# First recurrent stage of a four-layer network: one multiply moves to GpSimd, one gate moves into PSUM, and the second layer runs two chunks behind

## The chip, the cores and the metric

The kernel runs on one core of a Trainium2 chip. A core has a matrix engine (TensorE, PE in the rows), VectorE (DVE), ScalarE (ACT), GpSimd (POOL), a queue that starts transfers (SP), an on-chip memory SBUF that all of them reach, and PSUM, eight banks of 512 fp32 columns by 128 partitions into which TensorE writes. The metric is the device time of one execution in microseconds (us); lower is better. The time before is the median of three runs.

## The reference, cut to what matters

The program computes eight sublayers, each followed by a residual add and a layer norm. Only the first is touched: two minGRU layers, one after the other, over 4 sequences of 1024 tokens with 128 features.

```python
def _mingru_train(x, Wz, bz, Wh, bh):
    k = jnp.einsum('bsi,hi->bsh', x, Wz) + bz
    log_z = -jax.nn.softplus(-k)
    log_coeffs = -jax.nn.softplus(k)
    log_tilde_h = _log_g(jnp.einsum('bsi,hi->bsh', x, Wh) + bh)
    ...
    log_h = a_star + jax.lax.cumlogsumexp(log_values - a_star, axis=1)
    return jnp.exp(log_h)[:, 1:]
...
h1 = _mingru_train(x, Wz0, bz0, Wh0, bh0)
h2 = _mingru_train(h1, Wz1, bz1, Wh1, bh1)
...
x = _layernorm(x + h2, axis=-1)
```

Out of the logarithm this is h[t] = a[t] h[t-1] + z[t] g[t] with z = sigmoid(k), the update gate; a = sigmoid(-k) = 1 - z, the decay; and g, the candidate, which is max(u + 0.5, sigmoid(u)) for u = Wh x + bh. The state starts at 0.5 in each sequence.

## The kernel before, in words

The program is a list of parts (`stage1`, a fence, the first layer norm, a fence, `stage2`, ...). Each part gives each engine its own instruction stream; semaphores (`Sig` objects) order work between engines, and a fence lets no engine into the next part until four engines have drained. Within an engine instructions run in the order in which they are written.

`stage1` cuts the 4096 tokens into 8 chunks of 512 (two to a sequence) and does each chunk in each of the two layers l: 16 items (l, i), in the order of the list `seq`; p is an item's place in it. For each item

- TensorE projects the chunk with Wz and Wh into two PSUM banks, `PS[2 * (p % 4)]` and the one behind it. An fp32 product of 512 columns is two MATMUL rows in the trace, so one item is four MATMUL rows. Items of layer 1 read the states of layer 0 in `H1`.
- ScalarE (`scalar`) evaluates three sigmoids: a into `Ba`, z into `Bz`, sigmoid(u) into `Bs`. In the rows they are L203 with ps,SM (a) and ps,W (z and sigmoid(u)).
- VectorE (`dve`) forms the candidate g (L211), multiplies it by z (L208), and runs the recurrence as one scan instruction (L432), into `H1` or `Bh`.
- GpSimd (`pool`) adds the states of layer 1 to the residual stream `XT` (L212), 8 adds in all.

`Ba` to `Bh` have three buffers each, and PSUM holds the projections of four items. `seq` puts layer 1 of chunk i behind layer 0 of chunk i + 1. The first layer norm begins behind the fence, so behind the last of the eight adds.

Of the kernel before, what the change touches and what calls it, by code (L numbers as in the profile page):

```python
# [8 lines left out]
ALU = mybir.AluOpType  # L9
ACT = mybir.ActivationFunctionType  # L10
# [7 lines left out]
NCH = T // CH  # L18
# [114 lines left out]
def ch(ap, i, k=CH):  # L133
    return ap[:, i * k:(i + 1) * k]
# [16 lines left out]
def of(plan, step):  # L151
    return [a for s, a in plan if s == step]


def build(nc, wp, xT_d, sidx_d, cs_d, vecs_d, out_d):
# [3 lines left out]
    sem = Semaphores(lone)  # L159
# [21 lines left out]
    PS = [PSALL[:, i * 512:(i + 1) * 512] for i in range(8)]  # L181

    def w(name):
        r, o, c = at[name]
        return W[0:r, o:o + c]
# [5 lines left out]
    def mm(out, lhsT, rhs, start=True, stop=True, **k):  # L191
        return nc.tensor.matmul(out, lhsT, rhs, start=start, stop=stop, **k)  # L192
# [8 lines left out]
    def act(out, x, f, bias=0.0, scale=1.0, acc=None):  # L201
        if acc is None:
            return nc.scalar.activation(out, x, f, bias=bias, scale=scale)  # L203
        return nc.scalar.activation(out, x, f, bias=bias, scale=scale, accum_out=acc)  # L204
# [3 lines left out]
    tt = lambda o, a, b, op: nc.vector.tensor_tensor(o, a, b, op)  # L208
    ts = lambda o, a, s1, s2, op0, op1=None: (nc.vector.tensor_scalar(o, a, s1, s2, op0, op1) if op1 is not None  # L209
                                             else nc.vector.tensor_scalar(o, a, s1, None, op0))  # L210
    stt = lambda o, a, s, b, op0, op1: nc.vector.scalar_tensor_tensor(out=o, in0=a, scalar=s, in1=b, op0=op0, op1=op1)  # L211
    gtt = lambda o, a, b, op: nc.gpsimd.tensor_tensor(o, a, b, op)  # L212
# [37 lines left out]
    for k in LN_ALONE:  # L250
        p = ln_plans[k] = [("centre", (k, 0)), ("centre", (k, 1))]
# [108 lines left out]
    def stage1():  # L360
        ar = arena()
        H1 = ar(T)
        Ba, Bz, Bs, Bg, Bh = ([ar(512) for _ in range(3)] for _ in range(5))
        nb, bh5 = SM[:, 64:66], SM[:, 66:68]
        b = w("b_l0a")
        b2 = b.rearrange("p (l k) -> p k l", k=2)
        seq = []
        for i in range(NCH + 1):
            seq += [(0, i)] if i < NCH else []
            seq += [(1, i - 1)] if i > 0 else []  # L370
        bias = Sig(sem("s1_biases"), ("nb", "bh5"))
        zh = Sig(sem("s1_projected"), seq)
        sg = Sig(sem("s1_gates"), seq)
        gg = Sig(sem("s1_candidate"), seq)
        gz = Sig(sem("s1_update"), seq)
        hs = Sig(sem("s1_state"), seq)
        added = Sig(sem("s1_added"), range(NCH))
        before = lambda p, n: seq[p - n]

        def pe(e):  # L380
            e.wait_ge(s_w[0], 16)
            for p, (l, i) in enumerate(seq):
                if l == 0:
                    e.wait_ge(s_x[i // 2], 16)
                else:
                    e.wait_ge(*hs.at((0, i)))
                if p >= 4:
                    e.wait_ge(*sg.at(before(p, 4)))
                    e.wait_ge(*gg.at(before(p, 4)))
                x = ch(H1 if l else XT, i)  # L390
                mm(PS[2 * (p % 4)], w(f"Wz{l}"), x)
                mm(PS[2 * (p % 4) + 1], w(f"Wh{l}"), x).then_inc(*zh((l, i)))

        def scalar(e):
            e.wait_ge(s_w[0], 16)
            e.wait_ge(*bias.at("bh5"))
            for p, (l, i) in enumerate(seq):
                pz, ph = PS[2 * (p % 4)], PS[2 * (p % 4) + 1]
                e.wait_ge(*zh.at((l, i)))
                if p >= 3:  # L400
                    e.wait_ge(*hs.at(before(p, 3)))
                act(Ba[p % 3], pz, ACT.Sigmoid, bias=nb[:, l:l + 1], scale=-1.0)
                act(Bz[p % 3], pz, ACT.Sigmoid, bias=b[:, 2 * l:2 * l + 1])
                act(Bs[p % 3], ph, ACT.Sigmoid, bias=b[:, 2 * l + 1:2 * l + 2]).then_inc(*sg((l, i)))

        def dve(e):
            nc.vector.memset(eps, 1e-5).then_inc(s_eps, 1)
            nc.vector.memset(power, -0.5).then_inc(s_eps, 1)
            e.wait_ge(s_w[0], 16)
            ts(nb, b2[:, 0, :], -1.0, None, ALU.mult).then_inc(*bias("nb"))  # L410
            ts(bh5, b2[:, 1, :], 0.5, None, ALU.add).then_inc(*bias("bh5"))
            e.wait_ge(*bias.at("bh5"))
            for p, (l, i) in enumerate(seq):
                a, z, s, g = Ba[p % 3], Bz[p % 3], Bs[p % 3], Bg[p % 3]
                e.wait_ge(*sg.at((l, i)))
                if p >= 3:
                    e.wait_ge(*hs.at(before(p, 3)))
                stt(g, PS[2 * (p % 4) + 1], bh5[:, l:l + 1], s, ALU.add, ALU.max).then_inc(*gg((l, i)))
                e.wait_ge(*gg.at((l, i)))
                tt(g, g, z, ALU.mult).then_inc(*gz((l, i)))  # L420
                e.wait_ge(*gz.at((l, i)))
                if i % 2:
                    e.wait_ge(*hs.at((l, i - 1)))
                if l == 0:
                    h = ch(H1, i)
                    first = H1[:, i * 512 - 1:i * 512] if i % 2 else 0.5
                else:
                    h = Bh[i % 3]
                    first = Bh[(i - 1) % 3][:, 511:512] if i % 2 else 0.5
                    if i >= 3:  # L430
                        e.wait_ge(*added.at(i - 3))
                nc.vector.tensor_tensor_scan(h, a, g, first, ALU.mult, ALU.add).then_inc(*hs((l, i)))  # L432

        def pool(e):
            for i in range(NCH):
                e.wait_ge(*hs.at((1, i)))
                gtt(ch(XT, i), ch(XT, i), Bh[i % 3], ALU.add).then_inc(*added(i))
        return dict(pe=pe, dve=dve, act=scalar, pool=pool)


# [1386 lines left out]
    gates = of(moe_all, "gate")  # L1827
# [786 lines left out]
    def late_weights(n):  # L2614
# [5 lines left out]
        return sync  # L2620

    stages = [stage1, stage2, stage3, stage4, stage5, stage6, stage7, stage8]
    norms = {k: layernorm for k in LN_ALONE}
    parts = []
    for k in range(1, LAST + 1):
        s = stages[k - 1]()
# [156 lines left out]
```

## Time and profile before

| | |
|---|---|
| median of 3 runs | 2811.22 us (2810.33 to 2815.75) |
| profiled execution, its own time | 2796.67 us |
| its span, first to last instruction | 2794.9 us |
| first stage in it, start of the span to the end of its last add | 65.65 us |
| busy share of the span | PE 87%, DVE 68%, ACT 52%, POOL 35% |
| mean granted TensorE clock | 0.93 of full speed |

The span is the time between the first and the last instruction of one profiled execution. That execution was 14.6 us shorter than the median of the runs. The first stage is 65.65 of 2794.9 us, 2.3% of it.

### The profile page before, as it was taken

How to read it: one execution, taken by the hardware profiler on the slowest of the kernel's cores; microseconds unless marked ns; L12 is line 12 of the kernel's file. 1: busy time of each engine (PE TensorE's matmuls, PEld its weight loads, DVE VectorE, ACT ScalarE, POOL GpSimd, SP SyncE). 2: the span in 40 equal slices, each digit the busy share in tenths (PEclk: the TensorE clock that was granted, in tenths of full speed). 3: DMA queues.
4: the chain of work that ended last, by engine and by line, in shares of the span. 5: the costliest groups of instructions: out<-in, count | busy, mean ns of one | idle time of the engine just before them, and what ended most of it. 6: DMA issues, size and time to landing. Idle time of an engine off the chain costs nothing. (4 is left out here: it accounts for less than half of the span.)

```text
span 2794.9 us, 35013 instructions
## 1 busy us (share of the span) xinstructions
PE 2443.1 (87%) x12090; PEld 1758.5 (63%) x12090; DVE 1906.8 (68%) x3547; ACT 1459.8 (52%) x3081; POOL 974.4 (35%) x769
## 2 busy tenths in 40 slices
PE   5677778698999999999989999688888887999998
PEld 2554556586888888888867776233333333677776
DVE  6747555776666665666486665498888896866765
ACT  4321223597444444444355555555555553788787
POOL 1000000010222222222125555588888884222221
PEclk8678899899999999999989999799899887999999
DMA  4000000000000000000010000222222220000001
GB/s 174 0 1 0 1 1 1 1 1 16 1 1 1 1 1 1 1 1 1 14 48 1 1 8 1 62 80 81 80 80 80 80 82 18 1 1 1 1 1 31
DMA packets 31169, 66.85 MB, mean 24 GB/s; under 512 B 3200, under 2 KB 7312, under 8 KB 30480
## 3 DMA queue, kind: packets, MB, share of 16 engines
q1 hardware_dynamic: 30960, 64.59, 7.5%
q8 instruction: 96, 1.57, 0.2%
q14 instruction: 81, 0.66, 0.1%
q0 software_dynamic: 32, 0.02, 0.0%
HBM read 61.98 MB, written 2.62 MB: 23 GB/s over the span
## 5 line engine op out<-in xcount | busy, mean ns | idle before, releaser
L192 PE MATMUL ps<-TMPr 128*128 128x512 f32 (+6 forms) x3936 | 1030.1, 409 | 62.9 <-DVE TMPr L208 34.9
L192 PEld LDWEIGHTS ps<-TMPr 128*128 128x128 f32 (+4 forms) x3936 | 727.0, 191 | 378.0 <-issue 182.8
L212 POOL TENSOR_TENSOR TMP<-TMP 128x512 f32<-128x512 f32 (+2 forms) x480 | 618.6, 1313 | 689.2 <-ACT TMP L203 466.1
L192 PE MATMUL ps<-TMP 128*128 128x65 f32 (+4 forms) x4320 | 520.7, 288 | 1.2 <-DVE TMP L207 0.5
L192 PEld LDWEIGHTS ps<-TMP 128*128 128x128 f32 (+3 forms) x4320 | 477.9, 192 | 58.2 <-issue 16.3
L192 PE MATMUL ps<-TMP,W 128*128 128x512 f32 (+5 forms) x720 | 385.5, 664 | 119.6 <-POOL TMP L212 42.2
L203 ACT ACTIVATE TMP<-ps,W 128x256 f32<-128x256 f32 (+2 forms) x512 | 274.0, 580 | 353.7 <-DVE TMP L208 193.4
L208 DVE TENSOR_TENSOR TMP<-ps,TMP 128x512 f32<-128x512 f32 (+1 forms) x434 | 251.0, 601 | 133.7 <-ACT TMP L203 74.5
L192 PEld LDWEIGHTS ps<-TMP,W 128*128 128x128 f32 (+3 forms) x720 | 133.5, 203 | 294.4 <-issue 165.9
L203 ACT ACTIVATE TMPr<-ps,W 128x512 fp32r<-128x512 f32 x352 | 242.4, 689 | 109.9 <-PE ps L192 89.1
L212 POOL TENSOR_TENSOR XT<-XT,XK 128x512 f32<-128x512 f32 x128 | 175.2, 1369 | 318.6 <-DVE XK L211 305.1
L211 DVE SCALAR_TENSOR_TENSOR TMPr<-ps,SM,XK 128x512 fp32r<-128x512 f32 x256 | 190.1, 749 | 121.3 <-ACT XK L203 119.1
L206 ACT COPY TMP<-ps 128x260 f32<-128x260 f32 (+6 forms) x172 | 71.2, 418 | 256.4 <-PE ps L192 198.0
L203 ACT ACTIVATE ps<-TMP,SM 128x512 f32<-128x512 f32 x256 | 173.6, 693 | 48.7 <-DVE TMP L2516 47.8
L192 PE MATMUL ps<-Wr 128*128 128x512 f32 (+1 forms) x768 | 189.0, 364 | 9.1 <-DVE Wr L208 9.0
L203 ACT ACTIVATE TMP<-ps 128x512 f32<-128x512 f32 x144 | 86.0, 598 | 171.1 <-PE ps L192 170.9
L2516 DVE TENSOR_TENSOR_SCAN TMP<-ps,SM,TMP 128x512 f32<-128x512 f32 x128 | 156.3, 1264 | 6.8 <-ACT ps L203 6.7
L2516 DVE TENSOR_TENSOR_SCAN TMP<-ps,TMP 128x512 f32<-128x512 f32 x128 | 149.5, 1205 | 15.5 <-ACT ps L203 11.2
L212 POOL TENSOR_TENSOR TMPr<-TMP,TMPr 128x512 fp32r<-128x512 f32 x72 | 92.8, 1291 | 163.5 <-ACT TMPr L206 163.5
L199 PE MATMUL ps<-W,TMP 128*128 128x128 f32 (+2 forms) x720 | 120.0, 283 | 31.7 <-DVE TMP L208 21.5
L208 DVE TENSOR_TENSOR TMP<-ps,W 128x512 f32<-128x512 f32 (+1 forms) x145 | 97.5, 673 | 61.4 <-PE ps L192 60.4
L192 PEld LDWEIGHTS ps<-Wr 128*128 128x128 f32 x768 | 124.1, 194 | 22.1 <-issue 9.6
(186 smaller groups left out, 2700.0 us busy)
## 6 DMA issues: line engine op xcount, KB each, us to landing
TMP<-rows SPq DMA_DIRECT2D x168, 256.0 KB, 3.6
W<-wp SPq DMA_DIRECT2D x1, 4124.0 KB, 13.2
W<-wp SPq DMA_DIRECT2D x1, 3072.0 KB, 25.2
W<-wp SPq DMA_DIRECT2D x1, 2136.5 KB, 18.3
XT<-xT SPq DMA_DIRECT2D x4, 512.0 KB, 5.9
out<-XK SPq DMA_DIRECT2D x8, 256.0 KB, 2.3
W<-wp SPq DMA_DIRECT2D x1, 1993.0 KB, 14.1
W<-wp SPq DMA_DIRECT2D x1, 903.0 KB, 9.8
```

The costliest lines, as they stand in the source:

```text
L192: return nc.tensor.matmul(out, lhsT, rhs, start=start, stop=stop, **k)
L199: turn = lambda out, x, ident: nc.tensor.transpose(out, x, ident)
L203: return nc.scalar.activation(out, x, f, bias=bias, scale=scale)
L206: acopy = lambda o, a: nc.scalar.copy(o, a)
L208: tt = lambda o, a, b, op: nc.vector.tensor_tensor(o, a, b, op)
L211: stt = lambda o, a, s, b, op0, op1: nc.vector.scalar_tensor_tensor(out=o, in0=a, scalar=s, in1=b, op0=op0, op1=op1)
L212: gtt = lambda o, a, b, op: nc.gpsimd.tensor_tensor(o, a, b, op)
L2516: nc.vector.tensor_tensor_scan(Hb[q % 4], Ab[q % 3], Ub[q % 6], first, ALU.mult, ALU.add).then_inc(*h_dve((a, x)))
```

## The change

Three edits, all in `stage1`.

1. The multiply g z moves from VectorE to GpSimd. VectorE's stream is rewritten: a helper `candidate(p)` forms g of item p, and it is called for item p + 1 ahead of the scan of item p. GpSimd's stream has the 16 multiplies and, behind the multiply of item (1, i), the add of chunk i - 1.
2. ScalarE evaluates z first, then sigmoid(u), and last the decay a, which it writes back over the projection in PSUM. `Ba` goes. The decay waits for the new signal `up`, which says that z has been read out of the same bank and written. The scan reads the decay from PSUM. A bank is therefore free for TensorE only when the scan of the item four places earlier is done (before: when its sigmoids and its candidate were).
3. `seq` puts layer 1 of chunk i behind layer 0 of chunk i + 2.

```diff
@@ stage1
-        Ba, Bz, Bs, Bg, Bh = ([ar(512) for _ in range(3)] for _ in range(5))
+        Bz, Bs, Bg, Bh = ([ar(512) for _ in range(3)] for _ in range(4))
@@
-        for i in range(NCH + 1):
+        for i in range(NCH + 2):
             seq += [(0, i)] if i < NCH else []
-            seq += [(1, i - 1)] if i > 0 else []
+            seq += [(1, i - 2)] if i > 1 else []
@@
-        sg = Sig(sem("s1_gates"), seq)
+        up, sg = (Sig(sem("s1_" + n), seq) for n in ("update_gate", "gates"))
@@ pe
                 if p >= 4:
-                    e.wait_ge(*sg.at(before(p, 4)))
+                    e.wait_ge(*hs.at(before(p, 4)))
                     e.wait_ge(*gg.at(before(p, 4)))
@@ scalar
                 if p >= 3:
-                    e.wait_ge(*hs.at(before(p, 3)))
-                act(Ba[p % 3], pz, ACT.Sigmoid, bias=nb[:, l:l + 1], scale=-1.0)
-                act(Bz[p % 3], pz, ACT.Sigmoid, bias=b[:, 2 * l:2 * l + 1])
-                act(Bs[p % 3], ph, ACT.Sigmoid, bias=b[:, 2 * l + 1:2 * l + 2]).then_inc(*sg((l, i)))
+                    e.wait_ge(*gz.at(before(p, 3)))
+                act(Bz[p % 3], pz, ACT.Sigmoid, bias=b[:, 2 * l:2 * l + 1]).then_inc(*up((l, i)))
+                act(Bs[p % 3], ph, ACT.Sigmoid, bias=b[:, 2 * l + 1:2 * l + 2])
+                e.wait_ge(*up.at((l, i)))
+                act(pz, pz, ACT.Sigmoid, bias=nb[:, l:l + 1], scale=-1.0).then_inc(*sg((l, i)))
@@ dve
-            for p, (l, i) in enumerate(seq):
-                a, z, s, g = Ba[p % 3], Bz[p % 3], Bs[p % 3], Bg[p % 3]
-                e.wait_ge(*sg.at((l, i)))
+
+            def candidate(p):
                 if p >= 3:
                     e.wait_ge(*hs.at(before(p, 3)))
-                stt(g, PS[2 * (p % 4) + 1], bh5[:, l:l + 1], s, ALU.add, ALU.max).then_inc(*gg((l, i)))
-                e.wait_ge(*gg.at((l, i)))
-                tt(g, g, z, ALU.mult).then_inc(*gz((l, i)))
+                l = seq[p][0]
+                e.wait_ge(*sg.at(seq[p]))
+                stt(Bg[p % 3], PS[2 * (p % 4) + 1], bh5[:, l:l + 1], Bs[p % 3], ALU.add, ALU.max).then_inc(*gg(seq[p]))
+
+            candidate(0)
+            for p, (l, i) in enumerate(seq):
+                if p + 1 < len(seq):
+                    candidate(p + 1)
                 e.wait_ge(*gz.at((l, i)))
@@
-                nc.vector.tensor_tensor_scan(h, a, g, first, ALU.mult, ALU.add).then_inc(*hs((l, i)))
+                nc.vector.tensor_tensor_scan(h, PS[2 * (p % 4)], Bg[p % 3], first, ALU.mult, ALU.add).then_inc(*hs((l, i)))
@@ pool
-            for i in range(NCH):
+            def add(i):
                 e.wait_ge(*hs.at((1, i)))
                 gtt(ch(XT, i), ch(XT, i), Bh[i % 3], ALU.add).then_inc(*added(i))
+
+            for p, (l, i) in enumerate(seq):
+                e.wait_ge(*gg.at((l, i)))
+                gtt(Bg[p % 3], Bg[p % 3], Bz[p % 3], ALU.mult).then_inc(*gz((l, i)))
+                if l == 1 and i > 0:
+                    add(i - 1)
+            add(NCH - 1)
```

The order of the instructions on three engines shows where they come to stand. First VectorE at the start of the stage, before. L211 is the candidate, L208 the multiply, and the scan stands in this view as a SCALAR_TENSOR_TENSOR of L432; the semaphores in brackets are those of the `Sig` objects.

```order
L211 SCALAR_TENSOR_TENSOR TMP<-ps,SM,TMP 128x512 [waits s1_gates,s1_biases]
L208 TENSOR_TENSOR TMP<-TMP 128x512 [waits s1_candidate]
L432 SCALAR_TENSOR_TENSOR TMP<-TMP 128x512 [waits s1_update]
L211 SCALAR_TENSOR_TENSOR TMP<-ps,SM,TMP 128x512 [waits s1_gates]
L208 TENSOR_TENSOR TMP<-TMP 128x512 [waits s1_candidate]
L432 SCALAR_TENSOR_TENSOR TMP<-TMP 128x512 [waits s1_state,s1_update]
```

The same place after the change; the scan is L437 there and reads ps, the decay in PSUM.

```order
L211 SCALAR_TENSOR_TENSOR TMP<-ps,SM,TMP 128x512 [waits s1_gates,s1_biases]
L211 SCALAR_TENSOR_TENSOR TMP<-ps,SM,TMP 128x512 [waits s1_gates]
L437 SCALAR_TENSOR_TENSOR TMP<-ps,TMP 128x512 [waits s1_update]
L211 SCALAR_TENSOR_TENSOR TMP<-ps,SM,TMP 128x512 [waits s1_gates]
L437 SCALAR_TENSOR_TENSOR TMP<-ps,TMP 128x512 [waits s1_state,s1_update]
```

VectorE has two instructions an item in place of three, and the candidate of the next item stands in front of each scan. Now GpSimd's stream of the whole stage after the change; before, the stage had one row there, eight adds (XT<-XT,TMP). Rows with TMP<-TMP are the multiplies.

```order
L212 TENSOR_TENSOR TMP<-TMP 128x512 [waits s1_candidate] x6
L212 TENSOR_TENSOR XT<-XT,TMP 128x512 [waits s1_state]
L212 TENSOR_TENSOR TMP<-TMP 128x512 [waits s1_candidate] x2
L212 TENSOR_TENSOR XT<-XT,TMP 128x512 [waits s1_state]
L212 TENSOR_TENSOR TMP<-TMP 128x512 [waits s1_candidate] x2
```

From the seventh row on an add stands behind every second multiply, and the multiply behind it queues until the add is done. Last TensorE at the start of the stage, as a difference; rows that read XT are items of layer 0, rows that read TMP items of layer 1 (a count of 2 is one item here).

```order
-L192 MATMUL ps<-XT,W 128x512 x4
+L192 MATMUL ps<-XT,W 128x512 x6
 L192 MATMUL ps<-TMP,W 128x512 x2
 L192 MATMUL ps<-XT,W 128x512 x2
@@ -11,7 +11,5 @@
 L192 MATMUL ps<-XT,W 128x512 x2
-L192 MATMUL ps<-TMP,W 128x512 x2
-L192 MATMUL ps<-XT,W 128x512 x2
-L192 MATMUL ps<-TMP,W 128x512 x4
+L192 MATMUL ps<-TMP,W 128x512 x6
```

Three chunks of layer 0 are projected before the first of layer 1, and at the end of the stage three items of layer 1 follow each other where there were two.

## Rows read from the trace of the kernel before

**Rows 1.** Page: the span.

```profile
span 2794.9 us, 35013 instructions
```

**Rows 2.** Waits, 5 to 66 us: engine, line, waited for, us, times, longest.

```profile
ACT TMP L203 <- PE ps L192: 22.2, 8, 5.7
...
DVE TMP L211 <- ACT TMP L203: 14.0, 3, 8.2
```

**Rows 3.** Timeline, VectorE, 27 to 36 us: start, us, instruction.

```profile
28.02 1.28 DVE L432 TENSOR_TENSOR_SCAN TMP<-TMP 128x512 f32<-128x512 f32 x1
29.22 0.73 DVE L211 SCALAR_TENSOR_TENSOR TMP<-ps,SM,TMP 128x512 f32<-128x512 f32 x1
29.98 1.22 DVE L208 TENSOR_TENSOR TMP<-TMP 128x512 f32<-128x512 f32 x1
31.24 1.29 DVE L432 TENSOR_TENSOR_SCAN TMP<-TMP 128x512 f32<-128x512 f32 x1
...
33.20 0.69 DVE L208 TENSOR_TENSOR TMP<-TMP 128x512 f32<-128x512 f32 x1
33.93 1.22 DVE L432 TENSOR_TENSOR_SCAN TMP<-TMP 128x512 f32<-128x512 f32 x1
35.07 0.72 DVE L211 SCALAR_TENSOR_TENSOR TMP<-ps,SM,TMP 128x512 f32<-128x512 f32 x1
```

**Rows 4.** Timeline, GpSimd, whole stage: first two and last adds.

```profile
23.55 1.27 POOL L212 TENSOR_TENSOR XT<-XT,TMP 128x512 f32<-128x512 f32 x1 [23.10 <-DVE TMP L432]
29.39 1.27 POOL L212 TENSOR_TENSOR XT<-XT,TMP 128x512 f32<-128x512 f32 x1 [4.57 <-DVE TMP L432]
...
64.39 1.26 POOL L212 TENSOR_TENSOR XT<-XT,TMP 128x512 f32<-128x512 f32 x1 [4.53 <-DVE TMP L432]
```

**Rows 5.** Timeline, TensorE: items of the stage, and the layer norm's first.

```profile
5.45 6.71 PE L192 MATMUL ps<-XT,W 128*128 128x512 f32 x8 [5.45 <-DMA XT<-xT]
15.34 3.48 PE L192 MATMUL ps<-TMP,W 128*128 128x512 f32 x4 [3.19 <-DVE TMP L432]
18.66 1.88 PE L192 MATMUL ps<-XT,W 128*128 128x512 f32 x4
20.37 1.88 PE L192 MATMUL ps<-TMP,W 128*128 128x512 f32 x4
...
55.95 3.65 PE L192 MATMUL ps<-TMP,W 128*128 128x512 f32 x4 [3.91 <-DVE TMP L432]
65.77 0.58 PE L192 MATMUL ps<-W,XT 128*128 128x128 f32 x1 [6.17 <-POOLq L236]
```

**Rows 6.** Timeline, VectorE and ScalarE, first, middle and last items.

```profile
10.60 0.69 ACT L203 ACTIVATE TMP<-ps,SM 128x512 f32<-128x512 f32 x1
...
12.55 0.75 DVE L211 SCALAR_TENSOR_TENSOR TMP<-ps,SM,TMP 128x512 f32<-128x512 f32 x1 [8.21 <-ACT TMP L203]
...
14.06 1.22 DVE L432 TENSOR_TENSOR_SCAN TMP<-TMP 128x512 f32<-128x512 f32 x1
...
18.86 0.69 ACT L203 ACTIVATE TMP<-ps,SM 128x512 f32<-128x512 f32 x1 [4.68 <-PE ps L192]
20.58 0.70 ACT L203 ACTIVATE TMP<-ps,SM 128x512 f32<-128x512 f32 x1
...
54.61 1.28 DVE L432 TENSOR_TENSOR_SCAN TMP<-TMP 128x512 f32<-128x512 f32 x1
```

**Rows 7.** A later scan stage: scans from PSUM beside GpSimd multiplies.

```profile
L2516 DVE TENSOR_TENSOR_SCAN TMP<-ps,TMP x128: 1187/1204/1225, 1785.2 to 2272.1; 128x512 f32<-128x512 f32 x128
L2516 DVE TENSOR_TENSOR_SCAN TMP<-ps,SM,TMP x128: 1248/1259/1284, 1853.1 to 2332.4; 128x512 f32<-128x512 f32 x128
...
1852.57 18.12 POOL L212 TENSOR_TENSOR TMP<-TMP 128x512 f32<-128x512 f32 x14
```

**Rows 8.** Windows: us; PE, PEld, DVE, ACT, POOL busy; clock, DMA share, GB/s.

```profile
32.00:34.00 2.00, 1.42 (x4) 0.70 (x5) 1.93 (x4) 0.27 (x1) 0.00 (x0) 1.00 0.00 0
...
62.00:64.00 2.00, 0.00 (x0) 0.00 (x0) 1.93 (x3) 0.00 (x0) 0.00 (x0) 0.69 0.00 0
```

## The prediction

> **What bounds the kernel now.** I read the span first [rows 1] and then only the first stage, since the edits touch nothing else. In the waits of that stage VectorE stopped for ScalarE three times, 14.0 us in all, and 8.2 of these are the wait for the first sigmoids [rows 2, 6]. Everybody else waits for VectorE or for what VectorE released: the eight adds on GpSimd come at a fixed distance, 23.55, 29.39 and so on to 64.39, and each waits some 4.57 us for a scan [rows 4]. So the reader is to see a stage that is bound by VectorE's own list from about 20 to 59 us, with a start and an end bound by the chain from one item to the next.
>
> One pair of items (one of each layer) takes 5.85 us on VectorE, from the candidate at 29.22 to that at 35.07 [rows 3]. It holds two candidates of 0.73, two scans of 1.22 to 1.29, and two multiplies, one of 0.69 and one of 1.22. The two multiplies differ by 0.53 us for the same shape. The long one, 29.98 to 31.20, begins inside GpSimd's add of 29.39 to 30.66 and ends 0.54 us behind it; the short one at 33.20 has no add beside it [rows 3, 4]. So the add holds up this multiply, and the stage has six such multiplies.
>
> **What the change does to each engine's list**, by pair. VectorE loses both multiplies and the hold-up. An instruction begins 0.08 us before the end of the one ahead of it where nothing has to be waited for (28.02 plus 1.28 is 29.30, the next starts at 29.22) [rows 3]. Scans that read their first operand from PSUM stand in a later stage, beside running GpSimd multiplies of the same shape, with medians of 1.204 and 1.259 us [rows 7]. That is no longer than the 1.22 and 1.28 here, so I take them, and a pair is 2 x (0.73 - 0.08) + 1.12 + 1.18 = 3.6 us in place of 5.85.
>
> GpSimd gets two multiplies beside its add. Back to back, 14 of them took 18.12 us, 1.29 each, with scans running [rows 7]. Three a pair are 3.9 us. This engine had 1.27 of 5.85 us to do and becomes the fullest. ScalarE keeps three sigmoids an item, 18.86 to 20.58 is 1.72 us an item, 3.4 a pair [rows 6]. TensorE needs 1.71 an item at the 2.4 GHz level (18.66 to 20.37), 3.4 a pair, and twice that at 1.2 GHz (6.71 for the first two items, 3.4 each) [rows 5]. So four engines would have 3.4 to 3.9 us to do in each pair, and no list alone allows less than 3.9.
>
> The chain must be looked at too, since a bank is now given back only by the scan. From a scan's end to TensorE 0.06 (14.06 plus 1.22 to 15.34); TensorE to the first sigmoid of the item about 2.0 (20.58 is the start of the sigmoids of the projections that began at 18.66 and had to queue, so this is a little generous; the first item shows the same chain at the lower clock); sigmoids to candidate 1.95 (10.60 to 12.55); candidate and hand-over to GpSimd 0.82; multiply 1.29 and hand-over 0.09; scan 1.24. Together 7.5 us for four items, 3.75 a pair [rows 5, 6, 7]. The hand-over of 0.09 is the one from the scan that ends at 29.30 to the add at 29.39 [rows 3, 4]. This is under 3.9 too, but only just, so waits in program order will show. I laid all 16 items out by these durations, each instruction at the latest of its engine's last start plus pitch and of what it waits for. Laid out in the same way, the old order gives 64.4 us for the end of the last add. The trace has 65.65, and most of the difference lies at the last item, whose projections ran at the lower clock (3.65 us at 55.95) [rows 5].
>
> *The start.* Sigmoids of item 0 still begin at 10.60 and its candidate at 12.55 [rows 6]. But candidate 1 is now written ahead of scan 0, and it waits for the second item's sigmoids, so scan 0 starts at 15.3 and not at 14.06: 1.2 us lost. Meanwhile TensorE has projected (0,2) without waiting. (1,0) starts at 16.6, at the lower clock in my layout as at 15.34 before. The scan of (0,3) then starts at 26.6; before it started at 31.24 [rows 3]. Gain 4.6.
>
> *Four pairs.* From the scan of (0,3) to that of (0,7): 23.4 us before (31.24 to 54.61) [rows 3, 6]; in the layout 16.3, or 4.08 a pair. That is 0.2 over GpSimd's 3.9, because the add, queued between two multiplies, makes the next one up to 1.29 us late, and the scan behind it, the bank and the projections four places on with it. Gain 7.1.
>
> *The end.* From the scan of (0,7), 54.61, to the end of the last add, 65.65, were 11.0 us. Now this scan starts at 42.9. The projections of (1,7) wait for its end and start at 44.2, sigmoids run 46.3 to 48.1, the candidate follows at 48.2 and the scan of (1,6), written behind it, at 48.8; then the multiply 49.0 to 50.3, the scan to 51.7, and the add to 53.0. 10.1 us. Gain 0.9.
>
> Sum 12.6 us: the last add ends at 53.0 in place of 65.65. The layer norm, whose first product came at 65.77 [rows 5], and all behind it begin so much earlier. Nothing there waits for a load: transfers of weights are over at 32 us (share 0 from then on) [rows 8].
>
> Costs taken at nothing. The wait for `up`: z is written 0.7 us after its start, and sigmoid(u) occupies ScalarE until 1.2; that cover gone, it would be some 0.2 an item. The write of the decay over its own projection: no row has a sigmoid that reads and writes one bank. At the least it is 0.69 like the others [rows 6]; at the most I take reading and writing one after the other, 0.58 more (the pitch of a sigmoid, a third of 1.72). I take 0.69. By the upper bound the layout ends at 58.1, a gain of 7.5.
>
> One rule stands against this change. First the rows: the multiply took 0.69 us on VectorE alone and 1.29 on GpSimd [rows 3, 7]. If it stayed in the path of each item, 16 x 0.60 = 9.6 us would be lost, where my layout gains 12.6. The Trainium skill (GPSIMD Engine Reference, Engine selection) says to put elementwise multiplies on VectorE and not on GpSimd, which it calls about 2x slower for two inputs. The trace agrees on the ratio (1.9). By that rule the edit would be a loss; it does not ask whether VectorE is the fullest engine, as it is here.
>
> Base: the profiled execution took 2796.67 us for a span of 2794.9, so it would come to 2784.1. The runs' median is 14.6 above it; the gain is taken off the median: 2811.2 - 12.6 = 2798.6.
>
> **The rivals.** (a) *The decay's write costs its upper bound*: gain 7.5, 2803.7. Nothing in the trace speaks for it; no row rules it out. 7 in 100. (b) *TensorE stays at 1.2 GHz through the stage*. An item of projections is then 3.41, the chain of four items 9.2 and TensorE's own list 6.8 a pair, and the layout ends at 69.1: 3.4 later, 2814.7. For it speaks that the lower level is there at the start and again at 55.95 [rows 5]; against it that TensorE would be busy 3.4 of 4.1 us in place of 3.4 of 5.85, and the low stretches followed on gaps. 6 in 100. (c) *The gain is given back by the clock behind the stage.* All later work meets other phases of the clock; one low stretch costs some 1.7 us (3.65 against the 1.88 of other items) [rows 5]. Four more of them leave 5.8, 2805.4, and five leave 4.1, 2807. Half of its 8 in 100 lies on each side of the bound. (d) *Slower: the multiply stays in the path.* It decides if the sigmoids of item p + 1 come only when scan p has ended; then candidate, multiply and scan stand in a row with no work of VectorE beside them, 9.6 us lost, 2820.8. Against it: three items' sigmoids are evaluated ahead, and ScalarE's 1.72 an item is under the 2.0 of the cycle. 3 in 100. (e) *More*: TensorE ran without a pause from 5.45 and goes on now at 12.2 [rows 5]; if it is at 2.4 GHz from there, the layout ends at 51.2, and if the layer norm also begins at that level, some 2 us more go: 2795. 6 in 100. At 62 to 64 us the clock fell with TensorE idle [rows 8], and it will be idle for some 7 us there again, so I do not expect the second part.
>
> **How the numbers follow.** My forecast, a gain of 10 to 15, has 70 in 100, and its own range is 2796 to 2801. A measurement of this kernel tells about 0.2% (5.6 us) from no change. Faster by more: the forecast, (a), (e) and half of (c), 87 in 100. Within: (b) and half of (c), 10. Slower: (d), 3. The runs of before spread from 2810.33 to 2815.75, so a few us are to be added to each side: the range is 2793 to 2807. It leaves out (b) and (d), some of (c), and scatter.
>
> **What would show it.** Right: the last add ends near 53 us; GpSimd's rows on the multiply are 1.26 to 1.30 long and at 4.1 us a pair; no 1.22 us instruction other than scans on VectorE; its scans 1.20 to 1.26. VectorE now idles in each pair, for sigmoids and for GpSimd. Wrong: sigmoids of form ps<-ps longer than 0.75; MATMUL items of 3.4 us in mid-stage; a pair over 4.5 us; or an unchanged end of the stage. If the stage ends at 53 and the total does not follow, (c) holds.

## The result and the profile after

| | before | changed |
|---|---|---|
| median of the runs | 2810.15 us (8 runs, 2802.81 to 2815.75) | 2798.27 us (8 runs, 2796.15 to 2808.41) |
| ratio, with its 95% interval | | 0.9967 (0.9954 to 0.998) |
| span of the profiled execution | 2794.9 us | 2795.1 us |
| end of the last add of the first stage in it | 65.65 us | 52.61 us |

The changed kernel is faster by 0.2 to 0.46%. The medians differ by 11.9 us (12.6 were forecast), the ratio means 9.3 us (5.6 to 12.9 by its interval). In a second set of runs the changed kernel had 2798.6 us and a ratio of 0.9962 (0.995 to 0.9975). And yet the two profiled executions have the same span, although the first stage is 13.0 us shorter. Two questions, then: is the stage shorter for the reasons given, and where are the 13 us in the pair of profiles?

The timeline of VectorE in the changed kernel shows one pair of mid-stage and the end. L211 is the candidate, L437 the scan.

```profile
34.22 1.28 DVE L437 TENSOR_TENSOR_SCAN TMP<-ps,TMP 128x512 f32<-128x512 f32 x1 [0.17 <-POOL TMP L212]
35.52 0.75 DVE L211 SCALAR_TENSOR_TENSOR TMP<-ps,SM,TMP 128x512 f32<-128x512 f32 x1
36.19 1.27 DVE L437 TENSOR_TENSOR_SCAN TMP<-ps,TMP 128x512 f32<-128x512 f32 x1
37.38 0.73 DVE L211 SCALAR_TENSOR_TENSOR TMP<-ps,SM,TMP 128x512 f32<-128x512 f32 x1
38.02 1.22 DVE L437 TENSOR_TENSOR_SCAN TMP<-ps,TMP 128x512 f32<-128x512 f32 x1
...
47.86 0.75 DVE L211 SCALAR_TENSOR_TENSOR TMP<-ps,SM,TMP 128x512 f32<-128x512 f32 x1 [2.62 <-ACT ps L203]
48.53 1.21 DVE L437 TENSOR_TENSOR_SCAN TMP<-ps,TMP 128x512 f32<-128x512 f32 x1
49.99 1.28 DVE L437 TENSOR_TENSOR_SCAN TMP<-ps,TMP 128x512 f32<-128x512 f32 x1 [0.25 <-POOL TMP L212]
```

From one scan of a layer to the next [rows 3] had six instructions, one of them held up (28.02 to 33.93, 5.9 us). Here two candidates and two scans fill the time from 34.22 to 38.02, 3.8 us, with stops of up to 0.2 us. The end has the stop of 2.6 us for the sigmoids of the last item, written ahead of the scan of (1,6).

GpSimd in the same kernel; TMP<-TMP are multiplies and XT<-XT,TMP adds.

```profile
36.59 1.28 POOL L212 TENSOR_TENSOR TMP<-TMP 128x512 f32<-128x512 f32 x1
38.19 1.27 POOL L212 TENSOR_TENSOR TMP<-TMP 128x512 f32<-128x512 f32 x1 [0.32 <-DVE TMP L211]
39.41 1.27 POOL L212 TENSOR_TENSOR XT<-XT,TMP 128x512 f32<-128x512 f32 x1
40.64 1.27 POOL L212 TENSOR_TENSOR TMP<-TMP 128x512 f32<-128x512 f32 x1
...
51.35 1.26 POOL L212 TENSOR_TENSOR XT<-XT,TMP 128x512 f32<-128x512 f32 x1 [0.18 <-DVE TMP L437]
```

Each is 1.26 to 1.28 us long, and back to back they start every 1.22 us. The last one ends at 52.61; in [rows 4] it ended at 65.65. The windows of the changed kernel (busy PE, PEld, DVE, ACT, POOL, then the clock) show how full the four engines are:

```profile
16.00:20.00 4.00, 3.60 (x6) 1.62 (x7) 2.18 (x3) 1.04 (x3) 1.82 (x2) 0.69 1.05 449
...
30.00:43.00 13.00, 10.83 (x24) 3.66 (x22) 12.46 (x14) 12.09 (x21) 11.91 (x11) 1.00 0.09 36
43.00:53.00 10.00, 2.71 (x5) 0.95 (x6) 5.40 (x6) 1.95 (x4) 7.97 (x7) 0.59 0.00 1
```

From 30 to 43 us VectorE is busy for 12.5 of 13 us, ScalarE for 12.1 and GpSimd for 11.9. No single one is the bound. From 43 to 53 us nothing is full: that is the chain of the last items.

### The profile page after: what moved, and what is told of

It reads as the page before. It is cut to its first block and busy times, and to the rows that moved or that the text cites. A ratio compares the mean times of both kernels' runs of the same rounds, so it can differ in the third digit from the quotient of the medians.

```text
span 2795.1 us, 35014 instructions
## 1 busy us (share of the span) xinstructions
PE 2455.2 (88%) x12090; PEld 1768.1 (63%) x12090; DVE 1893.9 (68%) x3531; ACT 1461.3 (52%) x3081; POOL 995.1 (36%) x785
## 5 line engine op out<-in xcount | busy, mean ns | idle before, releaser
L212 POOL TENSOR_TENSOR TMP<-TMP 128x512 f32<-128x512 f32 (+2 forms) x496 | 639.2, 1314 | 714.6 <-ACT TMP L203 468.5
L208 DVE TENSOR_TENSOR TMP<-ps,TMP 128x512 f32<-128x512 f32 (+1 forms) x434 | 251.2, 603 | 134.0 <-ACT TMP L203 73.9
L211 DVE SCALAR_TENSOR_TENSOR TMPr<-ps,SM,XK 128x512 fp32r<-128x512 f32 x256 | 190.2, 750 | 122.2 <-ACT XK L203 119.9
L208 DVE TENSOR_TENSOR TMP<-ps,W 128x512 f32<-128x512 f32 (+1 forms) x145 | 97.6, 673 | 61.6 <-PE ps L192 60.6
## 6 DMA issues: line engine op xcount, KB each, us to landing
W<-wp SPq DMA_DIRECT2D x1, 4124.0 KB, 13.5
```

## The experiments

All times are medians in us; "laid out" is what was forecast for the end of the stage, and "last add" is the end of the last add of the stage in the profiled execution. Each kernel was timed beside the kernel before: lag_alone to decay_in_sbuf with its median at 2809.23, candidate_in_place, padded_stage and the first of three chunks at 2809.83, the second of the changed kernel and of three chunks and four chunks at 2807.67. So between variants of different sets the ratios compare better than the medians.

| kernel | laid out | last add | median | ratio (95%) |
|---|---|---|---|---|
| changed | 53.0 | 52.61, again 52.17 | 2798.27, again 2798.6 | 0.9967, again 0.9962 |
| lag_alone | 61 | 60.36 | 2804.53 | 0.9982 (0.9972 to 0.9993) |
| one_chunk_behind | 68.7 | 73.73 | 2815.2 | 1.002 (1.001 to 1.0029) |
| multiply_on_vector | 62 to 64 | 64.63 | 2811.7 | 1.0004 (0.9994 to 1.0013) |
| decay_in_sbuf | 65 | 64.41 | 2806.48 | 0.9997 (0.9979 to 1.0016) |
| candidate_in_place | 67 to 68 | 66.59 | 2812.26 | 1.0008 (0.9995 to 1.0021) |
| padded_stage | 64.9 (end of the padding) | 64.96 | 2808.16 | 0.9993 (0.9981 to 1.0004) |
| three_chunks_behind | 51.2 | 47.69, again 47.95 | 2790.76, again 2795.39 | 0.9931, again 0.9958 |
| four_chunks_behind | 48 to 50 | 48.28 | 2793.54 | 0.995 (0.993 to 0.997) |
| before_again | | 64.65 | 2809.29 (one run) | |

**The order of items alone** (edit 3 in the kernel before).

```diff
-        for i in range(NCH + 1):
+        for i in range(NCH + 2):
             seq += [(0, i)] if i < NCH else []
-            seq += [(1, i - 1)] if i > 0 else []
+            seq += [(1, i - 2)] if i > 1 else []
```

> The kernel before with only the order of items changed: layer 1 runs two chunks behind layer 0. My theory is that the stage is laid out by the engines' lists and the chain from item to item. VectorE's list is the bound in mid-stage and stays as it is, 5.85 us a pair with the multiply held up by the add, so the mid-stage does not move; only the start loses its stop of some 3 us before the third item, and a little goes at the end. Last add at 61 us, where before has 65.65 and the changed kernel 52.6. The rival, that the longer distance between the layers is what gives most of the gain, expects 53 to 56.

60.36 us. The mid-stage stays VectorE's: from the scan of (0,3) to that of (0,7) it takes 23.4 us, as before. VectorE's two other stops are gone, the one at the start (2.76 us in the first profile of the kernel before, 2.58 in the second) and the one for the last item (3.00 and 2.10). The gain is 5.3 us against the first profile and 4.3 against the second, which ends at 64.65. The first theory holds.

**All but the order of items.** The same lines the other way round, in the changed kernel.

> The changed kernel with the old order of items, layer 1 one chunk behind. Multiply on GpSimd, decay in PSUM and the candidate ahead of the scan stay. My theory: the projections of (1, i) wait for the scan of (0, i), which now comes two items earlier in the list and not five, and the candidate of the next item is written ahead of the scan, so the chain of about 7.5 us is paid once a pair or nearly so (5.9 us a pair). Last add at 68.7 us, later than before, so all of the gain and 3 us more are lost. The rival, that the multiply on GpSimd gives the gain and the distance only trims the start, expects 56 to 58.

73.73 us, 9.1 later than in the second profile of the kernel before (64.65). The sign is as expected, and the size is 5 us more. VectorE's timeline shows a stop for sigmoids in every pair:

```profile
34.68 0.75 DVE L211 SCALAR_TENSOR_TENSOR TMP<-ps,SM,TMP 128x512 f32<-128x512 f32 x1 [3.83 <-ACT ps L203]
...
40.62 0.75 DVE L211 SCALAR_TENSOR_TENSOR TMP<-ps,SM,TMP 128x512 f32<-128x512 f32 x1 [2.22 <-ACT ps L203]
```

This pair is 5.94 us (34.68 to 40.62), as laid out (5.9), but every second one is longer. TensorE has the reason, in two rows out of eight of this kind:

```profile
36.67 1.99 PE L192 MATMUL ps<-TMP,W 128*128 128x512 f32 x4 [2.24 <-DVE TMP L437]
...
42.55 3.68 PE L192 MATMUL ps<-TMP,W 128*128 128x512 f32 x4 [2.18 <-DVE TMP L437]
```

It stands idle for 2.2 us in each pair, and the projections behind the stop took 3.65, 3.68, 3.53 and 3.48 us in four cases behind 20 us, the rate of 1.2 GHz, which my layout did not have. Four times 1.5 to 1.7 us are 6.4, and the miss is 5.0. So the other edits together are worth nothing, and less, while layer 1 follows one chunk behind. Which of them costs the time there was not taken apart.

**The multiply back on VectorE.**

```diff
+                e.wait_ge(*gg.at((l, i)))
+                tt(Bg[p % 3], Bg[p % 3], Bz[p % 3], ALU.mult).then_inc(*gz((l, i)))
                 e.wait_ge(*gz.at((l, i)))
...
             for p, (l, i) in enumerate(seq):
-                e.wait_ge(*gg.at((l, i)))
-                gtt(Bg[p % 3], Bg[p % 3], Bz[p % 3], ALU.mult).then_inc(*gz((l, i)))
```

> The changed kernel with the multiply back on VectorE, right ahead of its scan; decay in PSUM, candidate ahead and the distance of two chunks stay. My theory: VectorE's list is the bound again, with two multiplies of 0.69 a pair, one of them held up by the add on GpSimd. Last add at 62 to 64 us, of 52.6. The rival, that freeing a bank late or the chain sets the pace in the changed kernel so that VectorE has slack for the multiply, expects under 56.

64.63 us: 12.0 us are gone with the multiply alone. One pair on VectorE:

```profile
35.11 1.22 DVE L439 TENSOR_TENSOR_SCAN TMP<-ps,TMP 128x512 f32<-128x512 f32 x1
...
36.89 0.68 DVE L208 TENSOR_TENSOR TMP<-TMP 128x512 f32<-128x512 f32 x1
...
39.39 1.34 DVE L208 TENSOR_TENSOR TMP<-TMP 128x512 f32<-128x512 f32 x1
40.77 1.28 DVE L439 TENSOR_TENSOR_SCAN TMP<-ps,TMP 128x512 f32<-128x512 f32 x1
```

VectorE is busy for 12.86 of the 13 us from 30 to 43, so it has no slack for the multiply, and one multiply in each pair is again held up by the add (1.34 us in place of 0.68). A pair takes 5.7 us, near the 5.85 of the kernel before.

**The decay in SBUF.**

```diff
+        Ba = [ar(512) for _ in range(4)]
...
-                act(pz, pz, ACT.Sigmoid, bias=nb[:, l:l + 1], scale=-1.0).then_inc(*sg((l, i)))
+                act(Ba[p % 4], pz, ACT.Sigmoid, bias=nb[:, l:l + 1], scale=-1.0).then_inc(*sg((l, i)))
...
-                nc.vector.tensor_tensor_scan(h, PS[2 * (p % 4)], Bg[p % 3], first, ALU.mult, ALU.add).then_inc(*hs((l, i)))
+                nc.vector.tensor_tensor_scan(h, Ba[p % 4], Bg[p % 3], first, ALU.mult, ALU.add).then_inc(*hs((l, i)))
```

> The changed kernel with the decay written to SBUF (four buffers) in place of PSUM, so that the scan reads two operands from SBUF; all else stays. Theory one: a VectorE instruction with two SBUF inputs and a GpSimd instruction that reads SBUF exclude each other, as the multiply and the add did in the kernel before; the scans and the three GpSimd instructions then share one time line of 2.4 plus 3.8 us a pair, and the last add is at 65 us, with scans or GpSimd rows that begin late or are longer than 1.3 us. Theory two: the hold-up is of the multiply instruction alone and not of the scan; then nothing moves, 52.6, and writing the decay to PSUM is worth nothing.

64.41 us. Theory one has the end to within 0.6 us, and theory two is out. First VectorE, then GpSimd, of this variant:

```profile
38.71 2.27 DVE L438 TENSOR_TENSOR_SCAN TMP<-TMP 128x512 f32<-128x512 f32 x1 [0.46 <-POOL TMP L212]
40.90 0.72 DVE L211 SCALAR_TENSOR_TENSOR TMP<-ps,SM,TMP 128x512 f32<-128x512 f32 x1
41.55 1.58 DVE L438 TENSOR_TENSOR_SCAN TMP<-TMP 128x512 f32<-128x512 f32 x1
43.05 0.72 DVE L211 SCALAR_TENSOR_TENSOR TMP<-ps,SM,TMP 128x512 f32<-128x512 f32 x1
44.23 2.27 DVE L438 TENSOR_TENSOR_SCAN TMP<-TMP 128x512 f32<-128x512 f32 x1 [0.46 <-POOL TMP L212]
```

```profile
36.48 3.42 POOL L212 TENSOR_TENSOR TMP<-TMP 128x512 f32<-128x512 f32 x2
39.86 2.19 POOL L212 TENSOR_TENSOR XT<-XT,TMP 128x512 f32<-128x512 f32 x1
42.01 3.41 POOL L212 TENSOR_TENSOR TMP<-TMP 128x512 f32<-128x512 f32 x2
```

The same scan is 1.58 and 2.27 us long in place of 1.21 and 1.27, and the GpSimd instructions are 2.19, or 3.42 for two, in place of 1.27 and 2.50; the candidate, with one operand in PSUM, keeps its 0.72. This is what the Trainium skill says (SBUF — State Buffer, Who interferes with whom): a VectorE instruction with two SBUF inputs and a GpSimd instruction that reads SBUF exclude each other for their whole length. The trace agrees here for the scan, as it did for the multiply before. A pair takes 5.52 us (38.71 to 44.23), where the shared time line was laid out at 6.2, so the mechanism holds and its terms were somewhat too large; that the end fits so well is in part chance.

**The candidate right ahead of its scan.**

```diff
-            candidate(0)
             for p, (l, i) in enumerate(seq):
-                if p + 1 < len(seq):
-                    candidate(p + 1)
+                candidate(p)
```

> The changed kernel with VectorE's list in the old order: the candidate of an item right ahead of its own scan, not one item earlier; multiply on GpSimd, decay in PSUM and two chunks of distance stay. My theory: VectorE now stands idle while GpSimd multiplies, so candidate, multiply and scan stand in a row (0.74, 0.08, 1.27, 0.08, 1.2, some 3.3 us an item and more where an add is queued ahead of the multiply). Last add at 67 to 68 us, later than before: the multiply's price on GpSimd is then paid. The rival, that the gates are ready early enough for GpSimd to work ahead anyway, expects under 56.

66.59 us. VectorE between two scans:

```profile
32.44 0.72 DVE L211 SCALAR_TENSOR_TENSOR TMP<-ps,SM,TMP 128x512 f32<-128x512 f32 x1
34.54 1.22 DVE L435 TENSOR_TENSOR_SCAN TMP<-ps,TMP 128x512 f32<-128x512 f32 x1 [1.38 <-POOL TMP L212]
```

Each of the 16 scans waits 1.37 or 1.38 us for GpSimd. This is the rival in which GpSimd's longer multiply is paid, made real: it comes about when VectorE has nothing else to do meanwhile.

**What lies behind the stage.** The changed kernel with ten idle multiplies at the end of GpSimd's list:

```diff
             add(NCH - 1)
+            for j in range(10):
+                gtt(pad[j], H1[:, 0:512], H1[:, 512:1024], ALU.mult)
```

> The changed kernel with ten more GpSimd multiplies of 128 by 512 at the end of the stage, written to fresh buffers that nobody reads, so that the stage ends at 64.9 us, about where it ended before. If what lies behind the stage costs the same wherever the stage ends, the total is 12.3 us above the changed kernel and level with the kernel before (2808 to 2812). If the time behind the stage depends on where the stage ends (the rival, the clock's turn after it), the total is well off that, and a part of the gain or loss of the changed kernel is of that kind.

2808.16 us, 9.9 above the changed kernel and 1.7 below the kernel before in the same set of runs, a ratio that tells no difference (0.9981 to 1.0004). The stage is 12.35 us longer than in the changed kernel. By the medians, which come from different sets of runs, 9.9 of these are in the total; by the ratios (0.9993 less 0.9967 or 0.9962) it is 7 to 9. So most of the time in the first stage reaches the total, and that up to 5 us of it do not is not excluded.

**A second profile of the kernel before.**

> The kernel before, unchanged, for a second profile. If its first profile, 14 us under the median of its runs, was a quick one, the second one has stage 2 (behind the first layer norm) some 6 us longer, as the changed kernel and the four variants have it, with more time at the lower clock. If the shorter later stages belong to a stage that ends at 65 us, they are the same again as in the first profile.

The first profile of before was a quick execution: of the 78 timed runs of that kernel only one was under 2797 us. The second took 2809.29 us, 12.6 more than the first (2796.67). One timeline row from each of three kernels' profiles (before, before again, changed) marks the start of stage 2, and a second the first product of the next layer norm:

```profile
83.06 0.45 PE L192 MATMUL ps<-W 64*128 64x1 f32 x2 [0.83 <-DVEq L228]
177.03 3.84 PE L192 MATMUL ps<-W,XT 128*128 128x128 f32 x32 [0.90 <-DVEq L228]
```

```profile
82.34 0.58 PE L192 MATMUL ps<-W 64*128 64x1 f32 x2 [0.83 <-DVEq L228]
182.53 5.77 PE L192 MATMUL ps<-W,XT 128*128 128x128 f32 x32 [0.90 <-DVEq L228]
```

```profile
70.34 0.58 PE L192 MATMUL ps<-W 64*128 64x1 f32 x2 [0.83 <-DVEq L228]
170.51 5.75 PE L192 MATMUL ps<-W,XT 128*128 128x128 f32 x32 [0.90 <-DVEq L228]
```

Stage 2 took 94.0 us in the first profile of before, 100.2 in the second, and 100.2 in the changed kernel. From there to the end of the span it is 2617.9, 2625.0 and 2624.6. So behind the first stage the changed kernel and the second profile of before agree to 0.4 us, and the first profile was 6.2 and 7 us quicker. The windows of 40 us that begin 56 us behind the start of stage 2 (the same three profiles; the first window reaches 2 us past the end of the stage) show another granted clock: 0.80 against 0.67 and 0.67.

```profile
139.00:179.00 40.00, 29.17 (x131) 19.99 (x132) 16.60 (x30) 10.26 (x29) 0.00 (x0) 0.80 0.00 0
```

```profile
138.00:178.00 40.00, 30.59 (x110) 19.13 (x111) 13.81 (x27) 9.63 (x23) 0.00 (x0) 0.67 0.00 0
```

```profile
126.00:166.00 40.00, 30.59 (x110) 19.09 (x111) 13.81 (x27) 9.64 (x23) 0.00 (x0) 0.67 0.00 0
```

One group of products is enough for the 6.2 us. In the groups of stage 2 (busy us, mean ns of one; before, then changed) sixteen rows take 7.1 us in one profile and 14.0 in the other:

```profile
L192 PE MATMUL ps<-TMP 64*128 64x512 f32 x16 | 7.1, 596 | 0.0
L192 PE MATMUL ps<-TMP 64*128 64x512 f32 x16 | 14.0, 1064 | 0.0
```

In the second profile of before they take 14.0 too. Nor is it a matter of the kernel before: of the 13 profiles on record, eleven have stage 2 at 100.1 to 102.3 us, and two at 93.8 and 94.0, the first of before and the first of three chunks behind. What decides which of the two an execution gets is not known.

**A second profile of the changed kernel.**

> The changed kernel, unchanged, for a second profile and more timings beside the other two of this call. By my theory (total = end of the first stage plus what lies behind it, which is the same for all variants within a few us) the last add is at 52 to 54 us and the median at 2796 to 2800. The rival, that the changed kernel's stage end moves with the clock by as much as three chunks gained, expects it anywhere from 49 to 53.

52.17 us and 2798.6. TensorE's projections behind the first scan took 1.98 and 1.88 us this time, 2.69 and 2.92 in the first profile, and the scan of (0,3) starts at 24.48 in place of 26.20. But the last item lost most of it again: its projections took 3.63 us here and 2.44 there, so the end of the stage moved by 0.4 us only.

```profile
41.84 3.63 PE L192 MATMUL ps<-TMP,W 128*128 128x512 f32 x4 [1.92 <-DVE TMP L437]
```

**More distance.** `NCH + 3` and `i - 3`, then `NCH + 4` and `i - 4`, in the same two lines of `seq`.

> The changed kernel with layer 1 three chunks behind layer 0. My theory: in mid-stage GpSimd's list of three instructions a pair (3.7 us) and the order of the lists set the pace and stay; the longer distance takes only the wait for the first scan at the start, some 1.4 us: last add at 51.2, total 1 us lower, which the timings cannot tell. The rival, that the distance is still the bound, expects under 49.

> Layer 1 three chunks behind, a second time. Its first profile ended the stage at 47.7 us, 4.9 ahead of the changed kernel, of which my layout gives 1.4 to the order of items and the rest to TensorE at 2.4 GHz from 12 us on: sixteen MATMUL rows without a pause and then a stop of 1.1 us, not 2.8. If that comes from the order of items, the stage ends at 47 to 49 us again and the median is 2789 to 2793. If it was chance, the stage ends at 51 and the median is near 2796.

47.69 us and 47.95, 3.5 and 3.3 less than laid out. The theory was short: my layout had TensorE at 1.2 GHz until 18 us, and here it was at 2.4 GHz from about 10 us to its last projection, both times. The windows of the first of these profiles, in which the clock is 1.00 from 16 to 20 us where the first profile of the changed kernel had 0.69:

```profile
5.00:16.00 11.00, 9.59 (x16) 3.88 (x16) 2.59 (x4) 6.71 (x11) 2.27 (x2) 1.00 1.04 430
16.00:20.00 4.00, 3.90 (x9) 1.65 (x10) 3.65 (x5) 3.45 (x7) 2.78 (x3) 1.00 1.00 425
```

The second profile of the changed kernel allows a comparison at one clock, since it too has 1.00 from 5 to 30 us. Its third scan starts at 20.91, the third scan of the second profile of three chunks at 18.71, and the fourteenth at 42.54 against 40.62: some 2 us are the stop at the start, and they stay. The stage then ends 4.2 us apart. The other 2.3 us are the last item. With two chunks its projections wait for the scan of (0,7), and TensorE, after 1.9 us without work, runs them at 1.2 GHz (3.63 us, where 1.98 is the other level); with three chunks they follow the ones ahead without a stop. So by this one pair of profiles 1.6 or 1.7 of the 4.2 us are the clock, and about 2.6 the order of items. The layout gives the same 2.6, with the upper level from 12.5 us on (48.4 for three chunks, 51.0 for two). The shorter pause of TensorE at the start (1.1 us with three chunks) is not needed to keep the clock up: in this profile of the changed kernel it stayed up after one of 2.5 us.

The total follows loosely. Three chunks had 2790.76 us in one set of runs and 2795.39 in the other, where the changed kernel had 2798.6. In that second set, the only one with both, the ratios are 0.9958 and 0.9962, and this difference can't be told from none.

> Layer 1 four chunks behind layer 0. My theory: the start has no stop left to take away beyond three chunks, while four items of layer 1 stand in a row at the end with an add each, so the last add is at 48 to 50 us, not earlier than with three, median 2790 to 2795. The rival, that each further chunk of distance gives time, expects 45.

48.28 us: not earlier than three, as expected.

Median less last add is 2745.7 and 2746.4 for the changed kernel, 2744.2, 2741.5, 2747.1, 2742.1, 2745.7, 2743.2, 2743.1, 2747.4 and 2745.3 for the others in the order of the table, and 2744.6 for the kernel before (2809.23 less 64.65, the last add of its second profile). The ends of the stage differ by 26 us, and what is behind it by 6.

## Why the prediction was right

**The bound.** That VectorE's list set the pace in mid-stage holds: with everything else changed and the multiply left there, the stage ends at 64.63 us.

**The sum.** The three parts of it, from the rows of the changed kernel (scan of (0,3) at 26.20, of (0,7) at 42.13): the start gained 5.0 us, of which 4.6 were forecast; the four pairs take 15.9 us, 3.98 a pair, and gained 7.4, with 7.1 forecast; the end takes 10.5 us, and gained 0.6, with 0.9 forecast. Together 13.0 for 12.6. Against the second profile of before the stage gained 12.0, and two profiles of one kernel differ by 0.3 to 1.0 us at its end, so the sum is right to about a microsecond. That the total, 2798.27 us, lies 0.3 from the 2798.6 of the forecast is luck beyond that: the median before moved from 2811.22 to 2810.15 with more runs, and the intervals of the two ratios leave 5.6 to 14 us for the gain.

**Terms that were a little off.** GpSimd's instructions start every 1.22 us back to back and not every 1.29, so its three come to 3.7 us a pair, and VectorE and ScalarE are as full as it is. The prediction called GpSimd the fullest and had VectorE idle in each pair; the window has VectorE ahead, busy for 12.5 of 13 us. So the pace of 3.98 for 4.08 us is close, and the account of what lies over GpSimd's list is not shown: the list was 0.2 shorter than in the sum, and the rest over it 0.1 longer. TensorE did reach the upper level, at about 10 us (three items in 7.87 us, where 3.4 each would be 10.2), and in the first profile fell back after its pause of 2.8 us. The clock column does not show its start: it reads 1.00 from 5 us on, while two projection rows start in each microsecond up to 10 us and four from 11 us on. The layout had the lower level until 18 us; rival (e) had the upper one from 12 us with an end at 51.2. The second profile of the changed kernel is that case, and it ends at 52.17 because of its slow last item.

**Costs taken at nothing.** The sigmoid that reads and writes one bank took 0.66 to 0.71 us, not more than the others, and where TensorE does not hold them up three sigmoids start every 1.72 us as before, so the wait for `up` is hidden. Rival (a) is out. Scans from PSUM took 1.21 to 1.28.

**The rival of the clock behind the stage, (c).** It describes the two profiles well: 13.0 us gained, then 13 given back against a quick execution. It does not describe the kernels: the second profile of before has none of it, and the padded kernel has the total of before to within 2 us. Only a small part of it stays possible: the ratios put the gain in the total at 9 to 11 us, the stage at 12 to 13.5. Had there been only the pair of profiles, this rival would have looked proven. The wrong piece of working here was to see that the profiled execution was 14.6 us under the median and not to say what would follow for the comparison of profiles.

**The rival on the other side, (d),** is real as a mechanism. With the candidate in its old place the stage ends at 66.59 us, 1.9 above the second profile of before, where the prediction had priced it at 9.6 with nothing else changed; the rest of the edits, which this variant keeps, can give back what lies between, but that was not taken apart. The rule of the Trainium skill against GpSimd for such multiplies (GPSIMD Engine Reference, Engine selection) therefore did not decide the sign; the ratio it gives is right (1.27 to 0.69), the work that stands beside the multiply decides.

What the prediction did not say is that the edits need one another. Taking back the order of items, the place of the candidate, the place of the multiply or the place of the decay, any one of them, puts the end of the stage at 64.4 us or later, where the second profile of before has 64.65. Of the edits only the order of items was tried alone; it is worth 4.3 to 5.3 us.

## What to carry to other kernels

In this stage moving work to a slower engine paid because three things came together: the engine that gave it up was the fullest, it had other work written ahead of the instruction that needs the result, and the recurrence left enough items in flight to cover the longer chain. Elsewhere, look for these three and test each by taking it back alone. GpSimd's instructions and VectorE instructions with two SBUF inputs held each other up here, and an operand in PSUM ended that. And before two profiles are compared, see where each stands among the timed runs of its kernel: here a second profile of the unchanged kernel showed that the first was the odd one, which the experiments on the change could only suggest.

## What the runs showed of the hardware that was not expected

- The exclusion of VectorE and GpSimd is seen from both sides: a scan with both inputs in SBUF is reported at 1.58 or 2.27 us in place of 1.21 to 1.28, and the GpSimd instruction at 2.19 in place of 1.27 (run decay_in_sbuf). In the rows shown each begins before the other has ended and itself ends 1.1 us behind that end, or 2.3 where two multiplies stand in one row.
- A sigmoid on ScalarE that reads and writes the same PSUM bank takes 0.67 us in the mean for 128 by 512, against 0.69 to SBUF, both before and in the variant with the decay in SBUF.
- One and the same program has stage 2 at 94.0 us in one execution and at 100.2 in another, and the same sixteen products at 596 and 1067 ns each. Three chunks behind has the same two ways (93.8 and 100.9 us). The length of the first stage does not decide it: with ends from 47.95 to 73.73 us stage 2 takes the longer time.
- TensorE's last projections of the stage ran at the lower level after a pause of 1.9 us in the second profile of the changed kernel, and those at its start stayed at the upper level after one of 2.5 us.
